# Three windowed-attention blocks and a spectral layer: load waits, places of the softmax inverses, and token order of the MLP in the 14-wide layers

## What is computed

```python
h = layer_norm(x, g1, beta1)
win, pad_hw = window_partition(h)
a = attention(win, w_qkv, b_qkv, w_proj, b_proj, rel_pos_h, rel_pos_w)
a = window_unpartition(a, pad_hw, (x.shape[1], x.shape[2]))
x = shortcut + a
h2 = layer_norm(x, g2, beta2)
mlp = gelu(h2 @ w_fc1 + b_fc1) @ w_fc2 + b_fc2
return x + mlp
# inside attention, per head:
attn = einsum('bhnd,bhmd->bhnm', q * SCALE, k) + rel_h[..., :, None] + rel_w[..., None, :]
out = softmax(attn) @ v            # then out @ w_proj + b_proj
```

## Time and profile before

| | us |
|---|---|
| median of 3 runs | 654.68 |
| lowest, highest | 652.26, 655.1 |
| the profiled execution | 650.77 |
| its span in the profile | 648.9 |

### The profile page before, as it was taken

The page is one execution under the profiler, slowest core; times in us unless marked ns, Lnnn a source line. Parts: engine busy times, 40 slices in busy tenths (PEclk is TensorE's granted clock), DMA queues, the critical chain, the costliest instruction groups (busy, mean ns, idle before and its releaser), DMA issues.

```text
span 648.9 us, 10072 instructions
## 1 busy us (share of the span) xinstructions
PE 569.5 (88%) x3792; PEld 414.2 (64%) x3792; DVE 300.7 (46%) x818; ACT 220.5 (34%) x443; POOL 156.7 (24%) x241
## 2 busy tenths in 40 slices
PE   7977885779998989899999899998988787799997
PEld 5737664564666675676767586665666565565776
DVE  3758674442132351445555634126586884500133
ACT  4214453424134024243353324135044564232120
POOL 7004132203004043151533305111051232210021
PEclk9996787797999998999999999999996998799999
DMA  6880456003312525635255403602824620200001
GB/s 175 217 197 23 115 115 157 2 2 96 87 46 79 103 75 123 158 78 108 77 124 142 120 1 85 144 0 64 171 51 107 139 79 2 62 1 0 1 0 49
DMA packets 22957, 54.75 MB, mean 84 GB/s; under 512 B 5842, under 2 KB 11578, under 8 KB 22814
## 3 DMA queue, kind: packets, MB, share of 16 engines
q1 hardware_dynamic: 20990, 53.79, 34.4%
q0 software_dynamic: 1920, 0.32, 0.4%
HBM read 11.53 MB, written 0.79 MB: 19 GB/s over the span
## 4 chain that ended last, share of the span: by engine, by line
PE 70%; DVE 12%; DMA 8%; issue 4%; SPq 3%; ACT 3%; POOL 1%; DVEq 0%; ACTq 0%
PE PS L1196 67%; DMA QA<-NR 5%; DVE NM L1090 5%; PE PS L1212 2%; DMA PT<-in_qm 1%; DMA QA<-REL 1%; SPq L674 1%; DVE HL L1103 1%; ACT REL L923 1%; DVE HL L1107 1%; DVE OT L1126 1%; SPq L675 1%; DVE REL L1077 1%; ACT HT L966 1%; PE PS L1289 1%
## 5 line engine op out<-in xcount | busy, mean ns | idle before, releaser
L1090 DVE TENSOR_REDUCE NM<-PS 98x2 f32<-98x392 f32 (+2 forms) x192 | 104.9, 568 | 82.5 <-PE PS L1196 81.0
L944 ACT ACTIVATE PT<-PS 98x392 f32<-98x392 f32 (+2 forms) x192 | 93.0, 516 | 81.8 <-PE PS L1196 78.3
L1196 PE MATMUL PS<-QA,KA 128*98 128x196 f32 (+2 forms) x480 | 94.2, 306 | 19.6 <-DMA QA<-NR 16.9
L1196 PE MATMUL PS<-KA,QA 126*98 126x196 f32 (+3 forms) x432 | 93.5, 314 | 13.5 <-DVE NM L1090 10.4
L1196 PEld LDWEIGHTS PS<-QA,KA 128*98 128x98 f32 (+2 forms) x480 | 71.7, 194 | 34.4 <-DMA QA<-NR 19.2
L1196 PEld LDWEIGHTS PS<-KA,QA 126*98 126x98 f32 (+3 forms) x432 | 63.1, 187 | 38.4 <-DVE NM L1090 19.7
L839 POOL DMA_DIRECT2D QA<-NR x60 | 34.3, 573 | 205.8 <-DVE NR L1114 205.6
L1196 PE MATMUL PS<-XT,W 96*128 96x512 f32 x144 | 68.6, 633 | 3.0 <-issue 3.0
L1196 PE MATMUL PS<-XT,WQKV 96*96 96x512 f32 x128 | 62.2, 617 | 5.3 <-issue 4.2
L1196 PE MATMUL PS<-PT,V 128*32 128x196 f32 (+2 forms) x672 | 56.9, 389 | 0.0
L1196 PE MATMUL PS<-W,HT 128*128 128x192 f32 x288 | 48.7, 328 | 4.7 <-ACT HT L966 4.7
(11 more groups left out here) (97 smaller groups left out, 678.6 us busy)
## 6 DMA issues: line engine op xcount, KB each, us to landing
QA<-QHL SPq DMA_DIRECT2D x36, 192.0 KB
KA<-KHL SPq DMA_DIRECT2D x24, 228.0 KB
QA<-REL SPq DMA_DIRECT2D x24, 224.0 KB
QA<-QHL SPq DMA_DIRECT2D x12, 384.0 KB
KA<-KHL SPq DMA_DIRECT2D x12, 384.0 KB
KA<-PT SPq DMA_DIRECT2D x12, 380.0 KB
W<-in_w SPq DMA_DIRECT2D x6, 576.0 KB, 5.3
QA<-REL SPq DMA_DIRECT2D x24, 128.0 KB
```

The lines of the kernel that those rows point to most:

```text
L944: nc.scalar.activation(dst, src, ACT.Exp).then_inc(probs_done.sem, 1)
L1090: nc.vector.tensor_reduce(dst, src, AX.X, ALU.max, negate=True).then_inc(max_done.sem, 1)
L1196: return nc.tensor.matmul(dst, lhsT, rhs, start=start, stop=stop, skip_group_check=loose)
```

## The change

Four things change, the first three in layers 0 and 2, the last at the border of layers 0 and 1.

1. The loads of the `weights` step wait as well for the rows of maxima of heads 10 and 11. The `WQKV` load stands behind them on SP.
2. `inverse` of the pairs 0 to 3 stands one unit of scores later, behind the `maxT` of an odd head instead of ahead of it, and `divide` one unit later. The place of pair 4 stays.
3. The MLP takes the tokens in two halves: tiles 0, 1, 4, 5 and tiles 2, 3, 6, 7. `proj`, `mid` and `ln` are done for one half and then for the other. `mlp_tiles` maps the k-th tile of the MLP to its tile of `X`.
4. Since `down` now delivers tile 2 and 3 as its fifth and sixth, `next_ln` of the tiles 0 to 3 stands behind two of the last four `down` steps and `next_turn` behind all of them.

```diff
+        self.mlp_tiles = [0, 1, 4, 5, 2, 3, 6, 7] if self.halves == 2 else list(range(TILES))
@@ windowed_attention
         for step, at, k in ((("copy_o", 1, 1) if tight else ("copy_o", 1, 4)),
-                            (("inverse", 1, 2) if tight else ("inverse", 1, 5)),
-                            (("divide", 1, 3) if tight else ("divide", 2, 1))):
+                            (("inverse", 1, 2) if tight else ("inverse", 2, 0)),
+                            (("divide", 1, 3) if tight else ("divide", 2, 2))):
@@ attention_steps
     if L.halves == 2:
-        out += [("proj", t, 0, t) for t in range(3)] + [("proj", t, 1, t) for t in range(3)]
-        out += [("proj", 3, u, 3) for u in range(2)]
-        out += [("mid", t, 0, t) for t in range(4)] + [("ln", 1, 0, 0)]
-        out += [("mid", t, 0, t) for t in range(4, TILES)] + [("turn", 1, 0, 0), ("ln", 1, 1, 0)]
+        for half in range(2):
+            out += [("proj", 2 * half + k, u, 0) for u in range(2) for k in range(2)]
+            out += [("mid", t, 0, L.mlp_tiles[t]) for t in range(4 * half, 4 * half + 4)]
+            out.append(("turn", 1, 0, 0) if half else ("ln", 1, 0, 0))
+        out.append(("ln", 1, 1, 0))
...
-        out += [("next_ln", 0, 0, 0), *down[:3], ("next_turn", 0, 0, 0), down[3], ("next_ln", 0, 1, 0)]
+        if L.halves == 2:
+            out += [*down[:2], ("next_ln", 0, 0, 0), *down[2:], ("next_turn", 0, 0, 0), ("next_ln", 0, 1, 0)]
+        else:
+            out += [("next_ln", 0, 0, 0), *down[:3], ("next_turn", 0, 0, 0), down[3], ("next_ln", 0, 1, 0)]
@@ sync, step "weights"
+                if L.pads:
+
+                    for h in (HEADS - 2, HEADS - 1):
+                        sp.wait_ge(*max_row_at(L, h))
                 sp.dma_start(m["W1"][:, :, :], io[f"w1_{n}"]).then_inc(mlp_in.sem, 16)
                 sp.dma_start(m["W2"][:, :, :], io[f"w2_{n}"]).then_inc(mlp_in.sem, 16)
@@ vector, step "ln"
+                source = L.mlp_tiles if s else range(TILES)
...
-                        dve.wait_ge(*x_end.at(n - 1, t))
-                    ins = nc.vector.bn_stats(STAT[:, t, :], X[:, t, :])
+                        dve.wait_ge(*x_end.at(n - 1, LAYERS[n - 1].mlp_tiles.index(t)))
+                    ins = nc.vector.bn_stats(STAT[:, t, :], X[:, source[t], :])
```

More of the change, by code:

```diff
@@ L849, in _ @@
                 pool.wait_ge(*xn_done.at(n, TILES + 4 * u + 3))
-                for t in range(4 * u, 4 * u + 4):
+                for t in L.mlp_tiles[4 * u:4 * u + 4]:
                     ins = nc.gpsimd.tensor_tensor(X[:, t, :], X[:, t, :], B2[n][:, :], ALU.add)
@@ L1018, in _ @@
                 for t in tiles:
-                    nc.vector.tensor_scalar(XN[:, t, :], X[:, t, :], MV[:, t, 0:1], RSTD[:, t:t + 1],
+                    nc.vector.tensor_scalar(XN[:, t, :], X[:, source[t], :], MV[:, t, 0:1], RSTD[:, t:t + 1],
                                             ALU.subtract, ALU.mult).then_inc(xn_done.sem, 1)
@@ L1147, in _ @@
             elif step == "mid":
-                dve.wait_ge(*proj_psum.at(n, i % (TILES // L.halves)))
-                nc.vector.tensor_tensor(X[:, i, :], X[:, i, :], PS[:, bank, 0:C], ALU.add).then_inc(x_mid.sem, 1)
+                t = L.mlp_tiles[i]
+                dve.wait_ge(*proj_psum.at(n, t % (TILES // L.halves)))
+                nc.vector.tensor_tensor(X[:, t, :], X[:, t, :], PS[:, bank, 0:C], ALU.add).then_inc(x_mid.sem, 1)
             elif step == "down":
@@ L1153, in _ @@
                 dve.wait_ge(*down_psum.at(n, i))
-                nc.vector.tensor_tensor(X[:, i, :], X[:, i, :], PS[:, bank, 0:C], ALU.add).then_inc(x_end.sem, 1)
+                x = X[:, L.mlp_tiles[i], :]
+                nc.vector.tensor_tensor(x, x, PS[:, bank, 0:C], ALU.add).then_inc(x_end.sem, 1)
         for u in range(1, 8, 2):
@@ L1377, in _ @@
                     for tile in tiles:
-                        claim(tile, x_mid.at(n, tile))
+                        claim(tile, x_mid.at(n, L.mlp_tiles.index(tile)))
                 groups = (L.groups - 1,) if u else range(L.groups - 1)
```

## The result

| | before | after |
|---|---|---|
| median of 4 runs, us | 653.47 | 628.07 |
| lowest, highest, us | 651.78, 655.1 | 625.79, 628.49 |
| the profiled execution, us | 650.77 | 625.79 |
| its span, us | 648.9 | 623.9 |

The ratio is 0.9581, with a 95% interval of 0.9532 to 0.963. The kernel is faster by 25.4 us by the medians and 25.0 by the spans, where 29.0 had been forecast. Two later comparisons gave the changed kernel medians of 634.24 and 632.41 us, against 659.47 and 655.79 before.

A forecast was written before the change was run, and what follows sets the result against it. TensorE was taken to bound the kernel, with 70% of the chain plus its stalls and the half clock behind them. 8.6 + 0.2 + 8.6 + 12.6 - 1.0 = 29.0 us off 654.7 gives 625.7, range 618 to 637.

The forecast's parts named there:

- Part 1: Layer 0, head 8: with weight loads held back, the 7.25 us stall and the half clock behind it go; 8.6 us.
- The 0.2 us for layer 2: Layer 2: the 0.53 us stall goes too, but DVE is nearly full there; 0.2 us counted, bounds 0 and 0.5.
- The rival that the row is late for its own reason: Row of maxima in layer 0: DMA queues served in turn, so holding loads gives near 0; 634.3 us, chance 0.06.
- Part 2: Last head's maxima, layers 0 and 2: stall shrinks from 3.4 to 1.2 us; with clock 8.6 us gained in all.
- layer 0's clock: Layer 0, last maxima transpose to scores of head 11: 6.76 us becomes 4.1 at full clock; 2.7 us gained.
- layer 2's clock: Layer 2, last maxima transpose to scores of head 11: 5.63 us becomes 4.1 at full clock; 1.5 us gained.
- at full clock I put it at 4.1: Layers 0 and 2: last maxima transpose to scores of head 11 takes 4.1 us, bounds 3.4 and 5.07.
- Part 3: MLP in halves, layers 0 and 2: first transposes 3.0 us earlier, work behind them at full clock; 12.6 us in all.
- The margin of the second layer norm: MLP, layer 0: the second half's layer norm is ready half a microsecond before the second transposes want it.
- The first rival: Whole kernel: new shorter pauses keep the clock down, so only 16.3 us is gained; 638.4 us, chance 0.15.
- Part 4: Border to layer 1: the gap after the transposes is no longer hidden; 1.0 us lost, 0.5 to 2.5.
- some 3 us either way: Half clock also comes and goes at places the change only shifts; worth some 3 us either way in the range.

The follow-up runs named there:

- part 1 alone: Kernel before, with only the loads of W1 and W2 in the 14-wide layers waiting for the rows of maxima of heads 10 and 11; ratio 0.9888.
- the pauses put back: Changed kernel with DVE's statistics of four MLP tiles computed twice or four times; projection to first MLP transposes 8.90 or 11.25 us, against 8.00.
- The short pause: Changed kernel with DVE's statistics of four MLP tiles computed twice; first to second MLP transposes 9.36 and 6.18 us in layers 0 and 2, against 5.91 and 5.90.

## Why the prediction was right, and where it was not

The forecast was 625.7 with a range of 618 to 637; the median is 628.07, and the two later medians, 634.24 and 632.41, lie in the range too. The stretches that the change aims at gave 27.5 us of 28.8 forecast for them. That the single terms agree to tenths is in part luck of the profile: forecast and result are both counted from the same execution of the kernel before, and other executions have the same stalls at other sizes. By the steps:

- **Part 1** (8.6 forecast, 8.8 seen in layer 0) is right in cause, and the experiment with part 1 alone shows it: T9 to T10 fell to 5.87 us there. Its size holds for the profiled execution, where the stretch was 14.50 us; against the 11.77 to 13.04 us of the three other traces with these loads it is 5.9 to 7.2. Taking the length from the same stretch of layer 2 was a good measure. The 0.2 us for layer 2 showed too: T9 to T10 there is 5.67 against 5.87.
- **The rival that the row is late for its own reason** (634) failed: the row landed within 0.7 us of the end of SP's traffic in five executions, and 1.6 to 2.7 us after its issue without that traffic. The rule that the prediction quotes from the Trainium skill ("DMA: Bandwidth & Descriptors", section "Queues, rings and completion order"), that an engine goes round its queues packet by packet, gives no such wait by itself. What makes the row wait here was not tried.
- **Part 2** is right in the stall (2.2 and 1.9 us) and in layer 0's clock (2.7; in the five other kernels that keep the stall T11 to P took 10.87 to 12.02 us in layer 0, so it is 1.5 to 2.6 against those). The term that was mis-sized is layer 2's clock: 1.5 forecast, 0.1 seen. The step "at full clock I put it at 4.1" holds (T11 to P is 9.4 us wherever the clock stays up), but in the changed kernel's layer 2 the clock did not stay up in any of the three executions that I read. In four other kernels with the same order on TensorE there, it did (9.38 to 9.40); the wait ahead of it was 1.50 and 1.51 us in two of them and 1.19 in the two with the pauses put back.
- **Part 3** is right in every term: 3.1 and 3.1 at the first transposes, 2.6 and 3.7 behind them, and it does so alone. (In the kernels without part 3, M1 to M2 took 8.32 to 9.92 us, so the second term is 2.4 to 4.0. A slip of the prediction costs nothing: four additions of 0.35 from 139.1 end at 140.5 and not at 140.3, and the transposes are ready when TensorE is, at 143.1.) The margin of the second layer norm was 1.0 us rather than 0.5. The first rival (the clock does not come back) failed here: transposes and a gap of 1.14 us left the clock up. The short pause shows how near it was: 0.83 us more idle time, and layer 0 went to half clock.
- **Part 4** cost 0.7 us where 1.0 had been put; the shorter second gap, which I had not counted, made it cheaper.
- **What was not forecast:** 2.2 us gained early in layer 0 and 4.7 lost from layer 1 to head 10 of layer 2. Of these 1.4 and 3.4 are half clock that came at other places, as the shift of "some 3 us either way" allowed for, though it came out on the wrong side. The rest of layer 1 and the way to the first head of layer 2 nearly cancel (1.6 us gained, 1.7 lost; the loss has half clock behind a wait of 1.31 us at 420 us). Another 1.2 us lie between the transposes for the heads 1 and 3 of layer 2. There the kernel before has a short step of DVE last 2.69 us beside an addition of POOL that began 0.15 us ahead of it, where it lasts 0.24 for other heads. In the changed one DVE comes 1.1 us ahead of POOL's addition, its step takes 1.23 us, and TensorE waits instead for the row that POOL issues behind the addition. Timeline of before, then of after:

```profile
478.42 2.75 POOL L817 TENSOR_TENSOR KHL<-OT,KHL 96x1216 fp32r<-96x1216 f32 x1
478.57 2.69 DVE L1107 TENSOR_TENSOR HL<-NM,HL 98x8 fp32r<-98x8 f32 x2
```

```profile
460.83 1.23 DVE L1118 TENSOR_TENSOR HL<-NM,HL 98x8 fp32r<-98x8 f32 x2
...
461.94 2.77 POOL L827 TENSOR_TENSOR KHL<-OT,KHL 96x1216 fp32r<-96x1216 f32 x1
...
464.67 2.72 POOL L849 DMA_DIRECT2D QA<-NR  x4
...
467.62 0.98 PE L1209 MATMUL PS<-QA,KA 128*98 128x196 f32 x4 [3.42 <-DMA QA<-NR]
```

  The two heads took 19.38 us against 18.14. In the fourteen traces, six have the pattern of the changed kernel's and took 18.7 to 19.7; of the eight with the pattern of before, seven took 18.1 to 18.7 and one 20.1. The changed kernel itself is on both sides (19.38, 19.24 and 18.40), and the kernel with W1 and W2 held back, which has none of the parts 2 to 4, took 19.36. So it varies between executions of one kernel, and it is no effect of these parts. What decides it was not tried.

Open is why the clock falls in layer 2 of the changed kernel and in layer 1 of some executions. A pause is not needed (184 to 191 us, TensorE busy throughout), and pauses of one length go either way: of five executions with 1.50 or 1.51 us ahead of the last transpose of layer 2, three fell and two did not. Yet length counts. With 1.19 or 1.20 us ahead of the last transpose of either layer the clock stayed up in all nine cases. Over all idle stretches of TensorE in the fourteen traces that began at full clock, the granted clock was below 1.00 within 4.5 us behind 6 of the 116 of 1.0 to 1.3 us, 66 of the 105 of 1.3 to 2 us, 26 of the 35 of 2 to 3 us, and all 37 of 3 us or more.

## What to carry to other kernels

Price a TensorE stall twice, as idle time and as half clock behind it, but count on the second part only for stalls of 3 us or more; from 1.3 to 3 us it came in most of the cases here and not in all, and below 1.3 us seldom. Read a stall's size from more than one execution before you price it: one and the same stretch took 11.8 to 14.5 us here. A large load issued ahead of a small transfer that someone waits for should be held back until that transfer has landed, if its own reader is far away. When a stall is filled, look at the next arrival in line and at how long before its use it is really issued: here it had been covered by the very stall.

## What the runs showed of the hardware that I had not expected

- The clock fell behind 37 of 37 idle stretches of 3 us or more, 66 of 105 of 1.3 to 2 us, and 6 of 116 of 1.0 to 1.3 us.
- A pause of 0.83 us ahead of the transposes, with the gap of 1.14 us behind them, brought the clock to 0.64 on average over the next 9 us in layer 0, and left it at 1.00 in layer 2, in one execution of one kernel.
- The clock fell to a mean of 0.62 over 7 us in which TensorE was busy for all 7.00.
- Rows of 8 KB on POOL's queue landed within 0.7 us of the 1.3 MB or more issued before them on SP's queue, 7.3 to 9.7 us after their own issue, in five executions; they took 3.1 to 3.4 us behind 1.2 MB in layer 2, and 1.6 to 2.7 us when SP's traffic was over.
